# Normalised rows on ScalarE and experts added in pairs, in the last stage of a gated attention block

## The chip, the cores and the metric

One core of a Trainium2 chip runs the kernel. The metric is the device time of one execution in microseconds, from its start to its end; the change is measured against the kernel before on the same chip.

## The reference, cut to what matters

A block with 32 sequences of 128 rows and 128 features, all f32. First a cross attention of 16 heads without mask adds to x. Then a second part with causal self attention, two layer norms and eight experts, of which the two best by gate count for each row:

```python
attn_out = ctx @ out_proj_w.T + out_proj_b
x1 = _layer_norm(x + attn_out, ln1_w, ln1_b)
gates = softmax(x1 @ gate_w.T + gate_b)
top_gates, top_idx = the two largest gates of each row
expert_outputs = einsum('bsd,efd->bsef', x1, expert_w) + expert_b
moe_out = sum over the two of expert_outputs * top_gates
return _layer_norm(x1 + moe_out, ln2_w, ln2_b)
```

The output is x + tanh(g_ffn) times this. The last stage of the kernel computes what stands here.

## The kernel before

The work is in groups of G = 2 sequences, 16 groups (GROUPS). Two attention stages fill the time up to about 372 us; every engine then goes through the last stage, the functions `z_pe`, `z_act`, `z_dve`, `z_pool` and `z_sp`. The change touches this stage alone.

The stage is a software pipeline. `z_steps` (line 684) runs `body(s, c)` on each engine for s from -1 to 20, and `in_z(c, lag)` says whether the group s - lag is in a part of the pipeline. So one step handles five groups, each in another part: the group 0 steps back has its attention copied, projected and added to x, the group 1 step back is normalised and multiplied with the first four experts, the group 2 back is gated, the group 3 back is summed, and the group 4 back gets its final norm. On an engine the order within a step is the order in `body`, written by hand. Engines hand over by semaphores that count groups.

For one group, from first to last:

- ScalarE `fetch` (799) copies the attention; PE `transpose_att` (714), ScalarE `copy_att` (806), PE `project` (724).
- VectorE `attention_sum` (859 to 866) adds and makes mean and variance z_mv. GpSimd `factor1` calls `rstd_of` (646 to 650): variance plus EPS, then the power -0.5 into z_rstd.
- VectorE `normalise1` (875) makes z_n, one tensor_scalar a sequence, from z_h, mean and z_rstd. GpSimd `x1` (970, 975) multiplies by the norm's weights and adds its bias. PE `transpose_n` (731), ScalarE `copy_x1` (813) with the same weights as scale and bias, PE `logits` (740).
- PE `experts` (752) multiplies by eight experts, four (HALF) at a time: k = 0 into s_bank0 and st_bank0, k = 1 into s_bank1 and st_bank1.
- VectorE `shift_logits` (883, 886), ScalarE `gates_exp` (819), VectorE `gating` (895 to 907): the two largest exponentials over the sum, z_gates. PE `gates_t` (762) and ScalarE `copy_gates` (827) transpose them for the experts' biases.
- VectorE `experts` (922) sums the first four experts, each times its gate, onto x1. ScalarE `gate_experts` (837) scales the other four into z_gated, waiting for PE's sum of the group before (`z_yb`). PE `gated_sum` (771, 773) adds the biases and, by a product with the identity, the four z_gated of each sequence: 8 f32 matmuls a group at line 773, each seen as two pieces in the profile.
- VectorE `all_experts` (933 to 940) adds both halves and makes mean and variance again. GpSimd `factor2` calls `rstd_of`, VectorE `normalise2` (947) makes z_y, GpSimd `final` (982, 985, 990) makes the output, and SyncE stores it (700).

The two `body` functions whose order matters are those of VectorE: shift_logits, normalise1, normalise2, gating, experts, attention_sum, all_experts; and of ScalarE: gates_exp, copy_att, copy_x1, fetch, gate_experts, copy_gates. GpSimd has final, x1, factor1, factor2.

## Time and profile before

| what | value |
|---|---|
| median of three runs | 520.43 us (519.47 to 521.97) |
| the profiled execution's own time | 522.93 us |
| its span, first to last instruction | 521.1 us |
| busy in the span: PE, VectorE, ScalarE, GpSimd | 448.9, 385.2, 278.6, 323.7 us |
| mean granted TensorE clock | 0.95 of full speed |
| first instruction of the last stage (z_att) | 372.0 us |

The profile names the engines PE (PEld for its weight loads), DVE (VectorE), ACT (ScalarE), POOL (GpSimd) and SP (SyncE). Busy time of an engine is the union of its instructions, which overlap on all of them but GpSimd, so that a group's busy time can be less than count times mean. The bracket behind an instruction in the timeline is the idle time before it and what ended it. Names such as z_rstd_ with an underscore at the end belong to the second norm, those without to the first.

### The profile page before, as it was taken

How to read it: one execution, taken by the hardware profiler on the slowest of the kernel's cores; microseconds unless marked ns; L12 is line 12 of the kernel's file. 1: busy time of each engine (PE TensorE's matmuls, PEld its weight loads, DVE VectorE, ACT ScalarE, POOL GpSimd, SP SyncE). 2: the span in 40 equal slices, each digit the busy share in tenths (PEclk: the TensorE clock that was granted, in tenths of full speed). 3: DMA queues.
4: the chain of work that ended last, by engine and by line, in shares of the span. 5: the costliest groups of instructions: out<-in, count | busy, mean ns of one | idle time of the engine just before them, and what ended most of it. 6: DMA issues, size and time to landing. Idle time of an engine off the chain costs nothing.

```text
span 521.1 us, 15905 instructions
## 1 busy us (share of the span) xinstructions
PE 448.9 (86%) x5728; PEld 280.0 (54%) x5728; DVE 385.2 (74%) x1191; ACT 278.6 (53%) x693; POOL 323.7 (62%) x702
## 2 busy tenths in 40 slices
PE   0369788778888899999999999999789999999983
PEld 0134444444444456666666666666447666666652
DVE  6377878787786777767777777773269899999981
ACT  1126656666565665666656666666444554554530
POOL 1445654565468898887888878621044766667654
PEclk9999979888797999999999999999879999999995
DMA  4565775556343434344343443420000000000000
GB/s 108 127 170 132 183 173 128 125 141 152 94 108 95 103 91 98 86 106 110 96 98 85 105 115 93 98 70 10 3 0 11 12 20 23 10 22 11 23 20 20
DMA packets 88333, 42.70 MB, mean 82 GB/s; under 512 B 16312, under 2 KB 88128, under 8 KB 88256
## 3 DMA queue, kind: packets, MB, share of 16 engines
q1 hardware_dynamic: 79040, 39.59, 30.8%
q10 hardware_dynamic: 9216, 2.10, 2.0%
q8 instruction: 46, 0.75, 0.6%
q14 instruction: 31, 0.25, 0.2%
HBM read 5.75 MB, written 2.10 MB: 15 GB/s over the span
## 4 chain that ended last, share of the span: by engine, by line
PE 32%; DVE 20%; POOL 17%; issue 6%; ACT 2%; POOLq 0%; ACTq 0%; DVEq 0%
PE u_bank L421 6%; DVE z_acc L922 5%; PE s_bank L374 4%; PE s_bank L364 4%; POOL xn_all L238 4%; PE u_bank L773 2%; POOL rstd L233 2%; PE u_bank L434 2%; PE s_bank L752 2%; DVE nm L599 2%; POOL rc L256 2%; PE st_bank L752 2%; PE t_bank L346 2%; POOL z_rstd_ L650 2%; DVE stats L555 1%
## 5 line engine op out<-in xcount | busy, mean ns | idle before, releaser
L599 DVE TENSOR_REDUCE nm<-s_bank 128x4 f32<-128x512 f32 x256 | 173.1, 684 | 73.5 <-PE s_bank L374 71.7
L499 ACT ACTIVATE pt<-st_bank 128x512 f32<-128x512 f32 x256 | 150.0, 598 | 102.6 <-PE st_bank L374 60.4
L374 PE MATMUL s_bank<-qk 64*128 64x128 bf16 x1024 | 105.7, 231 | 11.3 <-DVE nm L599 7.7
L421 PE MATMUL u_bank<-pt,vaug 128*32 128x128 f32 x2048 | 113.8, 296 | 0.0
L374 PE MATMUL st_bank<-qk 64*128 64x128 bf16 x1024 | 106.4, 227 | 0.0
L374 PEld LDWEIGHTS s_bank<-qk 64*128 64x128 bf16 x1024 | 70.7, 99 | 39.2 <-issue 27.7
L374 PEld LDWEIGHTS st_bank<-qk 64*128 64x128 bf16 x1024 | 71.4, 98 | 0.4
L421 PEld LDWEIGHTS u_bank<-pt,vaug 128*32 128x32 f32 x2048 | 41.4, 111 | 29.0 <-issue 4.1
L364 PE MATMUL s_bank<-mqk,esel 64*128 64x256 bf16 x256 | 49.7, 274 | 0.4 <-ACT pt L499 0.4
L364 PE MATMUL st_bank<-mkq,esel 64*128 64x256 bf16 x256 | 49.7, 274 | 0.0
L280 POOL TENSOR_TENSOR part<-r,part 128x512 bf16<-128x512 f32 x32 | 37.1, 1159 | 2.7
L773 PE MATMUL u_bank<-z_gated,idf 128*128 128x128 f32 x256 | 38.4, 295 | 0.0
L837 ACT ACTIVATE z_gated<-s_bank,z_gates 128x128 f32<-128x128 f32 x64 | 18.2, 368 | 35.7 <-PE u_bank L773 35.7
L346 PE MATMUL t_bank<-idf,xp 128*128 128x128 f32 x32 | 9.2, 382 | 31.7 <-DVE xp L565 18.2
L752 PE MATMUL s_bank<-ewt,z_x_t 128*128 128x512 f32 x64 | 35.2, 632 | 0.3 <-DVE z_acc L922 0.3
L773 PEld LDWEIGHTS u_bank<-z_gated,idf 128*128 128x128 f32 x256 | 32.1, 197 | 4.0 <-issue 0.2
L752 PE MATMUL st_bank<-ewt,z_x_t 128*128 128x512 f32 x64 | 33.5, 605 | 0.0
L291 POOL TENSOR_SCALAR mst<-nm 128x16 bf16<-128x16 f32 x64 | 13.0, 203 | 32.1 <-DVE nm L599 29.2
L301 POOL TENSOR_TENSOR x_all<-x_all,ao 128x128 f32<-128x128 f32 x32 | 14.6, 455 | 28.3 <-DVE ao L616 27.2
L506 ACT ACTIVATE mts<-m_bank 128x128 bf16<-128x128 bf16 x64 | 17.8, 278 | 26.4 <-PE m_bank L429 26.2
L434 PE MATMUL u_bank<-idf,us 128*128 128x128 f32 x128 | 30.2, 321 | 0.5 <-ACT us L515 0.5
L648 POOL TENSOR_SCALAR z_ve<-z_mv 128x2 f32<-128x2 f32 x16 | 3.1, 191 | 43.4 <-DVE z_mv L866 43.3
(118 smaller groups left out, 904.3 us busy)
## 6 DMA issues: line engine op xcount, KB each, us to landing
qk<-part SPq DMA_DIRECT2D x224, 128.0 KB, 2.6
x_all<-x SPq DMA_DIRECT2D x16, 128.0 KB, 2.6
c_all<-ctx_in SPq DMA_DIRECT2D x16, 128.0 KB, 2.8
qk<-qrow SPq DMA_DIRECT2D x32, 64.0 KB, 2.1
qk<-mts ACTq DMA_DIRECT2D x64, 32.0 KB, 2.6
out<-z_o SPq DMA_DIRECT2D x16, 128.0 KB, 1.8
ewt<-exp_t SPq DMA_DIRECT2D x1, 512.0 KB
qk<-krow SPq DMA_DIRECT2D x4, 64.0 KB, 2.0
```

The lines of the kernel that those rows point to most:

```text
L238: pool.tensor_scalar(one(xn2_all, u * G + b), one(x_all, u * G + b), mv[u % 2][:, b, 0:1], rstd[:, b:b + 1], ALU.subtract, ALU.mult).then_ ...
L280: pool.tensor_tensor(part[u % 2][:, 2:2 * PARTS:PARTS, :], r32[:, :].rearrange("c (o t) -> c o t", o=2), part[u % 2][:, 1:2 * PARTS:PARTS, ...
L346: ins = pe.transpose(t_bank[:, i * P:(i + 1) * P], a, idf[:, :])
L364: pe.matmul(to, esel[rows, block, :], mask[rows, rows].unsqueeze(1).broadcast_to([64, HEADS, 64]), start=block == 0, stop=False, skip_grou ...
L374: return pe.matmul(bank[:, j * P:(j + 1) * P], k if keys_first else q, q if keys_first else k, start=not masked, stop=True, skip_group_che ...
L421: ins = pe.matmul(u_bank[b][32 * j:32 * j + 32, r * P:(r + 1) * P], v, pt[m % 4][:, j, :], start=half == 0, stop=half == 1, skip_group_che ...
L434: ins = pe.transpose(u_bank[q % 2][:, W + r * P:W + (r + 1) * P], us[q % 2][:, r * P:(r + 1) * P], idf[:, :])
L499: act.activation(pt[m % 4][:, :, :].rearrange("k j q -> k (j q)"), st_bank[m % 2][:, :], ACT.Exp).then_inc(ex, 1)
L599: dve.tensor_reduce(nm[q % 2][:, first:first + HEADS], s_bank[n % 2][:, :].rearrange("q (j k) -> q j k", j=HEADS), AX_X, ALU.max, negate=T ...
L752: ins = pe.matmul(e_bank[b][k][:, :], zx1t[i][:, b * P:(b + 1) * P], ewt[:, k * 512:(k + 1) * 512], start=True, stop=True)
L773: ins = pe.matmul(dst, idf[:, :], zyg[:, b, e, :], start=False, stop=e == HALF - 1)
L922: dve.scalar_tensor_tensor(out=zacc[i][e % 2][:, b, :], in0=e_bank[b][0][:, e * P:(e + 1) * P], scalar=zg[i][:, b, e:e + 1], in1=zacc[i][( ...
```

## The change

On ScalarE, `normalise1` and `normalise2` compute z * rstd + offset, with offset = -mean * rstd, as an activation with scale and bias taken per row; before, VectorE computed (z - mean) * rstd. GpSimd makes the offset in two more instructions of 128x2 behind each power. On VectorE, `gated_pairs` adds the four z_gated of each sequence two and two, in one instruction of 128x512 for both sequences, and PE sums two terms a sequence instead of four. `gate_experts` waits for this pair sum of the group before and no longer for PE's sum; `gated_pairs` waits for PE's sum of the group before. On ScalarE normalise1 stands first in the step, normalise2 behind copy_att; on VectorE gated_pairs stands where the two normalise functions stood.

```diff
--- before.py
+++ after.py
@@ -643,11 +643,14 @@
                         values(s + 2)
 
 
-        def rstd_of(pool, v_in, v_eps, r_out, semaphore, k):
-
-            pool.tensor_scalar(v_eps, v_in, 1.0, EPS, ALU.mult, ALU.add).then_inc(semaphore, 1)
+        def factor_and_offset(pool, mean_var, v_eps, r_out, mean_r, offset, semaphore, k):
+            pool.tensor_scalar(v_eps, mean_var[:, :, 1], 1.0, EPS, ALU.mult, ALU.add).then_inc(semaphore, 1)
             pool.wait_ge(semaphore, k + 1)
             pool.tensor_tensor(r_out, v_eps, mhalf[:, :], ALU.pow).then_inc(semaphore, 1)
+            pool.wait_ge(semaphore, k + 2)
+            pool.tensor_tensor(mean_r, mean_var[:, :, 0], r_out, ALU.mult).then_inc(semaphore, 1)
+            pool.wait_ge(semaphore, k + 3)
+            pool.tensor_scalar(offset, mean_r, -1.0, 0.0, ALU.mult, ALU.add).then_inc(semaphore, 1)
 
         def two(name, shape):
             return [sb(f"{name}{i}", shape) for i in range(2)]
@@ -655,7 +658,7 @@
         zo_t = two("z_att_t", [P, W])
         zh = two("z_h", [P, G, P])
         zst = two("z_stats", [P, G, 6]); zmv = two("z_mv", [P, G, 2]); zve = two("z_ve", [P, G]); zrs = two("z_rstd", [P, G])
-        zn = two("z_n", [P, G, P])
+        zn = two("z_n", [P, G, P]); znb = two("z_offset", [P, G]); zmr = two("z_mean_r", [P, G])
         zw = sb("z_nw", [P, G, P]); zx1 = two("z_x1", [P, G, P])
         zx1t = two("z_x1_t", [P, W])
         zl = sb("z_logit", [P, G, NE]); zm = sb("z_max", [P, G]); zp = sb("z_exps", [P, G, NE])
@@ -664,15 +667,15 @@
         zt = sb("z_top", [P, G, NE]); zg = two("z_gates", [P, G, NE]); zgt = two("z_gates_t", [NE, W])
         zacc = [[sb(f"z_acc{i}{j}", [P, G, P]) for j in range(2)] for i in range(2)]
         zst2 = sb("z_stats2_", [P, G, 6]); zmv2 = sb("z_mv2_", [P, G, 2]); zve2 = sb("z_ve2_", [P, G])
-        zrs2 = sb("z_rstd2_", [P, G]); zy = sb("z_y2", [P, G, P]); zyw = sb("z_yw", [P, G, P])
-        zsum = sb("z_x1_moe", [P, G, P]); zyg = sb("z_gated", [P, G, HALF, P]); zyb = sb("z_ywb", [P, G, P]); zo = two("z_o", [P, G, P])
+        zrs2 = sb("z_rstd2_", [P, G]); znb2 = sb("z_offset2_", [P, G]); zmr2 = sb("z_mean_r2_", [P, G]); zy = sb("z_y2", [P, G, P]); zyw = sb("z_yw", [P, G, P])
+        zsum = sb("z_x1_moe", [P, G, P]); zyg = sb("z_gated", [P, G, HALF, P]); zyp = sb("z_gated_pairs", [P, G, HALF // 2, P]); zyb = sb("z_ywb", [P, G, P]); zo = two("z_o", [P, G, P])
 
         z_at = sem("z_att_copied"); z_ot = sem("z_att_transposed"); z_otc = sem("z_att_t_copied")
         z_proj = sem("z_projected"); z_h = sem("z_ln1_steps"); z_rs = sem("z_rstd_steps")
         z_n = sem("z_normalised"); z_x1 = sem("z_x1_steps")
         z_nt = sem("z_n_transposed"); z_x1c = sem("z_x1_t_copied"); z_lg = sem("z_logits_ready")
         z_gate = sem("z_gate_steps"); z_exp = sem("z_gate_exp"); z_gt = sem("z_gates_transposed")
-        z_gtc = sem("z_gates_t_copied"); z_y = [sem(f"z_experts{k}") for k in range(2)]; z_yg = sem("z_experts_gated"); z_yb = sem("z_expert_bias")
+        z_gtc = sem("z_gates_t_copied"); z_y = [sem(f"z_experts{k}") for k in range(2)]; z_yg = sem("z_experts_gated"); z_yp = sem("z_gated_pairs_summed"); z_yb = sem("z_expert_bias")
         z_acc = sem("z_accumulated"); z_all = sem("z_all_summed_steps"); z_rs2 = sem("z_rstd2_steps"); z_y2s = sem("z_normalised2")
         z_fin = sem("z_final_steps"); z_out = sem("z_stored")
         H1 = 1 + 2 * G
@@ -765,12 +768,12 @@
             def gated_sum(g, gc):
                 i = gc % 2
                 pe.wait_ge(z_gtc, g + 1)
-                pe.wait_ge(z_yg, g + 1)
+                pe.wait_ge(z_yp, g + 1)
                 for b in range(G):
                     dst = u_bank[0][:, b * P:(b + 1) * P]
                     pe.matmul(dst, zgt[i][:, b * P:(b + 1) * P], ebs[:, :], start=True, stop=False)
-                    for e in range(HALF):
-                        ins = pe.matmul(dst, idf[:, :], zyg[:, b, e, :], start=False, stop=e == HALF - 1)
+                    for e in range(HALF // 2):
+                        ins = pe.matmul(dst, idf[:, :], zyp[:, b, e, :], start=False, stop=e == HALF // 2 - 1)
                 ins.then_inc(z_yb, 1)
 
             def body(s, c):
@@ -813,6 +816,24 @@
                 act.activation(zx1t[i][:, :], t_bank[:, 0:W], ACT.Identity, bias=l1bc[:, :],
                                scale=l1wc[:, :]).then_inc(z_x1c, 1)
 
+            def normalise1(g, gc):
+                i = gc % 2
+                act.wait_ge(z_rs, (g + 1) * 4)
+                if gc >= 2:
+                    act.wait_ge(z_nt, g - 1)
+                    act.wait_ge(z_x1, (g - 2) * 2 + 1)
+                for b in range(G):
+                    act.activation(zn[i][:, b, :], zh[i][:, b, :], ACT.Identity, bias=znb[i][:, b:b + 1],
+                                   scale=zrs[i][:, b:b + 1]).then_inc(z_n, 1)
+
+            def normalise2(g, gc):
+                act.wait_ge(z_rs2, (g + 1) * 4)
+                if gc >= 1:
+                    act.wait_ge(z_fin, (g - 1) * FIN + 1)
+                for b in range(G):
+                    act.activation(zy[:, b, :], zsum[:, b, :], ACT.Identity, bias=znb2[:, b:b + 1],
+                                   scale=zrs2[:, b:b + 1]).then_inc(z_y2s, 1)
+
             def gates_exp(g, gc):
                 act.wait_ge(z_gate, g * GATE + 2)
                 for b in range(G):
@@ -831,7 +852,7 @@
                 act.wait_ge(z_gate, (g + 1) * GATE)
                 act.wait_ge(z_y[1], g + 1)
                 if gc >= 1:
-                    act.wait_ge(z_yb, g)
+                    act.wait_ge(z_yp, g)
                 for b in range(G):
                     for e in range(HALF):
                         ins = act.activation(zyg[:, b, e, :], e_bank[b][1][:, e * P:(e + 1) * P], ACT.Copy,
@@ -839,10 +860,14 @@
                 ins.then_inc(z_yg, 1)
 
             def body(s, c):
+                if in_z(c, 1):
+                    normalise1(s - 1, c - 1)
                 if in_z(c, 2):
                     gates_exp(s - 2, c - 2)
                 if in_z(c, 0):
                     copy_att(s, c)
+                if in_z(c, 4):
+                    normalise2(s - 4, c - 4)
                 if in_z(c, 1):
                     copy_x1(s - 1, c - 1)
                 if in_z(c, -1):
@@ -864,16 +889,6 @@
                 dve.wait_ge(z_h, g * H1 + 1 + G)
                 for b in range(G):
                     dve.bn_aggr(zmv[i][:, b, :], zst[i][:, b, :]).then_inc(z_h, 1)
-
-            def normalise1(g, gc):
-                i = gc % 2
-                dve.wait_ge(z_rs, (g + 1) * 2)
-                if gc >= 2:
-                    dve.wait_ge(z_nt, g - 1)
-                    dve.wait_ge(z_x1, (g - 2) * 2 + 1)
-                for b in range(G):
-                    dve.tensor_scalar(zn[i][:, b, :], zh[i][:, b, :], zmv[i][:, b, 0:1], zrs[i][:, b:b + 1],
-                                      ALU.subtract, ALU.mult).then_inc(z_n, 1)
 
             per_seq = [P, G, NE]
 
@@ -924,6 +939,13 @@
                             scalar=zg[i][:, b, e:e + 1], in1=zacc[i][(e + 1) % 2][:, b, :] if e else zx1[i][:, b, :],
                             op0=ALU.mult, op1=ALU.add).then_inc(z_acc, 1)
 
+            def gated_pairs(g, gc):
+                dve.wait_ge(z_yg, g + 1)
+                if gc >= 1:
+                    dve.wait_ge(z_yb, g)
+                dve.tensor_tensor(zyp[:, :, :, :], zyg[:, :, 0:HALF // 2, :], zyg[:, :, HALF // 2:HALF, :],
+                                  ALU.add).then_inc(z_yp, 1)
+
             def all_experts(g, gc):
                 k = g * ALL
                 dve.wait_ge(z_yb, g + 1)
@@ -939,21 +961,11 @@
                 for b in range(G):
                     dve.bn_aggr(zmv2[:, b, :], zst2[:, b, :]).then_inc(z_all, 1)
 
-            def normalise2(g, gc):
-                dve.wait_ge(z_rs2, (g + 1) * 2)
-                if gc >= 1:
-                    dve.wait_ge(z_fin, (g - 1) * FIN + 1)
-                for b in range(G):
-                    dve.tensor_scalar(zy[:, b, :], zsum[:, b, :], zmv2[:, b, 0:1], zrs2[:, b:b + 1],
-                                      ALU.subtract, ALU.mult).then_inc(z_y2s, 1)
-
             def body(s, c):
                 if in_z(c, 2):
                     shift_logits(s - 2, c - 2)
-                if in_z(c, 1):
-                    normalise1(s - 1, c - 1)
-                if in_z(c, 4):
-                    normalise2(s - 4, c - 4)
+                if in_z(c, 3):
+                    gated_pairs(s - 3, c - 3)
                 if in_z(c, 2):
                     gating(s - 2, c - 2)
                     experts(s - 2, c - 2)
@@ -994,11 +1006,11 @@
                 pool.wait_ge(z_h, (g + 1) * H1)
                 if gc >= 2:
                     pool.wait_ge(z_n, (g - 1) * G)
-                rstd_of(pool, zmv[i][:, :, 1], zve[i][:, :], zrs[i][:, :], z_rs, g * 2)
+                factor_and_offset(pool, zmv[i], zve[i][:, :], zrs[i][:, :], zmr[i][:, :], znb[i][:, :], z_rs, g * 4)
 
             def factor2(g, gc):
                 pool.wait_ge(z_all, (g + 1) * ALL)
-                rstd_of(pool, zmv2[:, :, 1], zve2[:, :], zrs2[:, :], z_rs2, g * 2)
+                factor_and_offset(pool, zmv2, zve2[:, :], zrs2[:, :], zmr2[:, :], znb2[:, :], z_rs2, g * 4)
 
             def body(s, c):
                 if in_z(c, 4):
```

## Rows read from the trace of the kernel before

**Rows 1.** Windows of one step: busy us (instructions) per engine, clock, DMA
```profile
452.80:460.87 8.07, 8.07 (x44) 5.50 (x43) 7.42 (x36) 4.13 (x16) 5.43 (x10) 1.00 0.05 16
```

**Rows 2.** Chain of waits in the last stage: start us, us, what
```profile
399.61 0.44 PE m_bank L724 x4
...
407.61 0.45 PE m_bank L724 x4
...
448.69 2.16 DVE z_acc L922 x8
...
456.75 2.16 DVE z_acc L922 x8
```

**Rows 3.** Timeline of one step, VectorE: start us, us, engine, line
```profile
453.01 0.14 DVE L883 TENSOR_TENSOR z_logit<-u_bank,gbb 128x16 f32<-128x16 f32 x1
...
453.29 0.60 DVE L875 TENSOR_SCALAR z_n<-z_h,z_mv,z_rstd 128x128 f32<-128x128 f32 x2
...
454.22 0.60 DVE L947 TENSOR_SCALAR z_y<-z_x_moe,z_mv_,z_rstd_ 128x128 f32<-128x128 f32 x2 [0.32 <-POOL z_rstd_ L650]
...
454.74 0.23 DVE L895 MAX8 z_sorted<-z_exps 128x8 f32<-128x8 f32 x2
...
455.00 0.65 DVE L898 COPY z_two<-z_sorted 128x4 f32<-128x4 f32 x1
...
459.80 0.25 DVE L866 BATCH_NORM_AGGREGATE z_mv<-z_stats 128x2 f32<-128x6 f32 x2
```

**Rows 4.** Groups by line, whole span: busy us, mean ns, idle before
```profile
L599 DVE TENSOR_REDUCE nm<-s_bank 128x4 f32<-128x512 f32 x256 | 173.1, 684 | 73.5 <-PE s_bank L374 71.7 <-POOL mst L291 1.0
...
L773 PE MATMUL u_bank<-z_gated,idf 128*128 128x128 f32 x256 | 38.4, 295 | 0.0
...
L293 POOL TENSOR_TENSOR mr<-nm,mst 128x16 f32<-128x16 f32 x64 | 13.9, 218 | 5.3
...
L933 DVE TENSOR_TENSOR z_x_moe<-u_bank,z_acc 128x256 f32<-128x256 f32 x16 | 6.4, 399 | 4.6 <-PE u_bank L773 4.5
```

**Rows 5.** Timeline of the same step, GpSimd
```profile
453.45 0.73 POOL L650 TENSOR_TENSOR z_rstd_<-z_ve_,mhalf 128x2 f32<-128x2 f32 x1
...
454.90 0.72 POOL L982 TENSOR_TENSOR z_yw<-z_y,l2w 128x256 f32<-128x256 f32 x1 [0.72 <-DVE z_y L947]
...
458.02 0.73 POOL L975 TENSOR_TENSOR z_x<-z_nw,l1b 128x256 f32<-128x256 f32 x1
...
460.14 0.19 POOL L648 TENSOR_SCALAR z_ve<-z_mv 128x2 f32<-128x2 f32 x1 [1.39 <-DVE z_mv L866]
...
460.41 0.70 POOL L650 TENSOR_TENSOR z_rstd<-z_ve,mhalf 128x2 f32<-128x2 f32 x1
```

**Rows 6.** Timeline of the same step, ScalarE
```profile
453.93 0.47 ACT L819 ACTIVATE z_exps<-z_logit,z_max 128x8 f32<-128x8 f32 x2
...
456.26 0.56 ACT L813 ACTIVATE z_x_t<-t_bank,l1bc,l1wc 128x256 f32<-128x256 f32 x1 [1.59 <-PE t_bank L731]
...
456.73 0.41 ACT L799 ACTIVATE z_att<-c_all 128x256 f32<-128x256 f32 x1
...
459.35 1.14 ACT L837 ACTIVATE z_gated<-s_bank,z_gates 128x128 f32<-128x128 f32 x4 [2.21 <-PE u_bank L773]
```

**Rows 7.** Lines 898 and 905: duration ns min/median/max, first and last start
```profile
L898 DVE COPY z_two<-z_sorted x16: 170/645/650, 381.5 to 502.7; 128x4 f32<-128x4 f32 x16
...
L905 DVE TENSOR_TENSOR z_top<-z_exps,z_others x16: 174/375/382, 382.4 to 503.4; 128x16 f32<-128x16 f32 x16
```

**Rows 8.** Timeline of the last groups
```profile
506.41 1.14 ACT L837 ACTIVATE z_gated<-s_bank,z_gates 128x128 f32<-128x128 f32 x4 [4.05 <-PE u_bank L773]
...
507.31 0.25 DVE L940 BATCH_NORM_AGGREGATE z_mv_<-z_stats_ 128x2 f32<-128x6 f32 x2
...
508.83 0.48 PE L771 MATMUL u_bank<-ebs,z_gates_t 8*128 8x128 f32 x2 [1.55 <-ACT z_gates_t L827]
...
511.45 2.08 PE L773 MATMUL u_bank<-z_gated,idf 128*128 128x128 f32 x8
```

## The prediction

> **What bounds the kernel now.** I read the windows first, to see which engines are full, then the chain of waits, to see which of them sets the end, then the timeline of one step of the last stage, to price what is moved. The stage runs from 372 us to the end and makes 16 groups in a software pipeline. One step in its middle lasts 8.07 us [rows 1]: PE is busy all of it, VectorE 7.42, GpSimd 5.43 and ScalarE 4.13. Two engines are thus nearly full at once. The chain says the same: up to 412 us it runs through PE, its project matmuls 8.00 us apart; later it runs through VectorE, its expert sums 8.06 apart [rows 2]. PE and VectorE each set the same period, so taking work from one alone gains nothing. The change takes from both, and what is left is a loop of handoffs.
>
> Within a step (t = 453.01, start of the logits' sum) [rows 3]: VectorE makes the first normalised rows at 453.29, waits for z_rstd_, makes the second at 454.22, starts the gating at 454.74 and the expert sums 2.01 later, at 456.75 [rows 2]. From there to the next step's logits (461.08) are 4.33 us.
>
> **The change, part by part.**
> PE loses 8 of its 16 pieces a group (an f32 matmul shows as two): 128 of the 256, whose busy time is 38.4 us in all [rows 4]. Half of it over 16 groups is 1.2 us a step, and PE's work becomes 8.07 - 1.2 = 6.9 us.
>
> VectorE loses both pairs of tensor_scalar and the wait between them: 454.74 - 453.29 = 1.45 us. It gains one sum of 128x512 (the four gated experts of each sequence, two and two, for both sequences at once). No row has a two-tensor sum so wide; the reduce over 512 columns takes 0.684 and z_x_moe over 256 takes 0.399 [rows 4]. These bound it at 0.68 and 2 x 0.40 = 0.80; I take 0.69, as its width is that of the reduce. VectorE's own work becomes 8.07 - 1.45 + 0.69 = 7.3 us.
>
> GpSimd gains two small instructions for each factor. The nearest is mr, 128x16, 0.218 us [rows 4]; z_ve, with 2 columns, takes 0.19 [rows 5]. With the 0.08 between dependent instructions (460.14 + 0.19 to 460.41) [rows 5] I take 0.29 + 0.27 = 0.56, between 0.54 and 0.60. A factor then takes 0.27 + 0.78 + 0.56 = 1.61 us until the next one can start, and 1.53 to the end of its last instruction.
>
> ScalarE gains four activations of 128x128 with two pointer operands. ScalarE has room, so their price is latency. z_x_t, with two pointers and 256 columns, takes 0.56 and the next starts 0.47 after it; z_gated, with one pointer and 128 columns, has starts (1.14 - 0.37) / 3 = 0.26 apart [rows 6]. For a pair, starts lie between 0.52 and 0.94 and the end between 0.61 and 1.03; between these I take starts 0.72 in all, and 0.82 to the end. The Trainium skill (ScalarE: Activation LUTs, What ACT_TABLE_LOAD costs) states 186 ns + 0.833 ns a column, 93 ns for each pointer operand and an overlap of 93 ns; that gives 0.77 and 0.87, and would add 0.05 to the sum below, which goes by the rows.
>
> What stands behind the new waits: the exponentials of the gating now queue behind normalise1 on ScalarE, and normalise1 waits for GpSimd's four instructions. VectorE's gating waits for the exponentials, and the attention sum that feeds the next factor comes after gating and experts. So the price of a handoff comes back in every step: attention sum, factor1, normalise1, exponentials, gating, experts, next attention sum. The copy of the attention also queues behind, so PE's project starts late, but PE has over 1 us to spare. normalise2 waits for factor2 and holds copy_x1, fetch and the gated experts behind it; these have room, since ScalarE had idle stretches of 2.21 us before z_gated [rows 6].
>
> **The port.** Two tiny VectorE instructions with both operands in SBUF, the copy z_two and the difference z_top, take 0.170 and 0.174 at best, 0.645 and 0.375 as a rule [rows 7]. In the step, z_two (455.00) ends at 455.65 while GpSimd's z_yw ends at 455.62 [rows 3, 5]; it waited for GpSimd. The new sum reads two SBUF operands for 0.69 us, so it may hold up GpSimd as well. The trace has no row for that side: bounds are 0 and the sum's whole 0.69. The Trainium skill (SBUF — State Buffer, SBUF: two separate sides) calls the shared pair "an exclusive lock, not a bandwidth split", either side blocking the other for a whole instruction; by it the wait exists, and without it the result would be the first rival's. The row agrees for VectorE waiting, none shows GpSimd waiting. I take the wait as real, since the small cases show one.
>
> **The sum for a step.** z_mv of the attention sum ends at 460.05 and GpSimd starts 0.09 later [rows 3, 5], if it is free. GpSimd's own loop, without port waits, is: factor1 1.61, factor2 1.53, handoff 0.04 (z_rstd_ ends 454.18, z_y starts 454.22), ScalarE's pair 0.82, to z_yw 0.08, from z_yw to the end of x1 454.90 to 458.75 = 3.85, and 0.08 to the next factor [rows 3, 5]: 8.01 us. GpSimd is thus nearly full itself. In a step of 8.27, the result below, its x1 ends at t + 7.7, and factor1 starts 0.4 later than the 0.09 would have it. The product mean*rstd, 1.05 after that start, is then ready at 0.5 after the next t, while the pair sum runs (from t + 0.28 to t + 0.97). I let the product end 0.10 after the sum (between 0.03, as z_two did, and 0.22, the whole instruction). Then offset 0.27, handoff 0.04, two normalised 0.72, exponentials 0.47 [rows 6] and handoff 0.04: gating starts at t + 2.61. Gating shrinks, because GpSimd is waiting for ScalarE at that time: z_two falls by 0.48 and z_top by 0.20, so 2.01 becomes 1.33 (between 1.33 and 2.01). Step: 2.61 + 1.33 + 4.33 = 8.27, or 0.20 more than before. With every term at its low end it is 7.96; with every one at its high end 9.4, of which 0.68 is a gating held up as before and 0.42 the dearest activations. I don't expect these together, and take 8.8 as the upper side of the range.
>
> **Ends of the stage.** At the start, factor1 is on the path once: +0.56, and +0.2 for ScalarE's pair against VectorE's 0.60 = +0.8. At the end, z_gated of the last group waited 4.05 us for PE's previous sum [rows 8]; that wait becomes one for the pair sum, which comes early. The last pair sum then queues behind the previous group's statistics, ending 507.56 (about 0.2 earlier now), and adds 0.7: PE starts at 508.1 instead of 508.83. That last gated sum took until 513.53, or 4.70 us; the bias pieces keep about 1.2, and half of the other 3.5 goes, 1.75. Factor and pair then cost 0.56 + 0.2. Together -0.7 - 1.75 + 0.76 = -1.7. Net of both ends: -0.9 us (between +0.5, if the last sum halves only in part, and -2.5, if the last groups run freer, having fewer stages beside them).
>
> Between them lie about 12 steps under the loop, 16 less four in which the pipeline fills: 12 x 0.20 = +2.4. Sum +1.5. The profiled execution, 522.93 us with a span of 521.10, becomes 524.4; it stands 2.5 above the median of the three runs, 520.43, which becomes 521.9. A measurement can tell about 0.5%, 2.6 us, from no change.
>
> **Rivals.**
> First, GpSimd isn't held by the sum. The step is then GpSimd's own loop, 8.01, or 7.76 with the small instructions and ScalarE's pair at their lower price. 12 x -0.06 - 0.9 = -1.6, or 12 x -0.31 - 0.9 = -4.6: 518.8 to 515.8. For it: no row shows GpSimd held, and its instructions of 128x256 keep 0.72 [rows 5]. Against: VectorE's two small ones are held at the median [rows 7].
> Second, the other side: the port wait adds in full to the POOL loop. If the power instruction also holds the port, the pair sum starts only when it ends, and the product waits for the whole sum: 8.01 + 0.69 = 8.70. 12 x 0.63 - 0.9 = +6.7: 527.1. The step from which this side decides is 8.07 + (2.6 + 0.9) / 12 = 8.36. For it: GpSimd's loop is the tightest. Against: the z_n pair (one tensor from SBUF each, so only a hint) took 0.60 beside z_rstd_ and isn't drawn out [rows 3, 5].
> Third, the handoffs hide after all, and VectorE's own 7.3 us sets the step: 12 x -0.77 - 0.9 = -10.1: 510.3. Against: gating can't start before the exponentials, and these follow normalise1; the order is in the code. The change would do nothing of what it says if PE's row of pieces did not halve; nothing speaks for that.
>
> **Chances.** Forecast 0.45 (of it 0.32 within 0.5%, 0.10 slower, 0.03 faster), first rival 0.27 (0.17 faster, 0.10 within), second 0.23 (all slower), third 0.05 (faster). Faster 0.25, same 0.42, slower 0.33. The range, 515.5 to 527.0, takes in the first rival and the forecast's bounds, and most of the second; it leaves out the third and the second's far end. The forecast's own is 519.5 to 525.
>
> **What would show it.** u_bank from z_gated: 128 pieces. PE busy under 90% of a step. VectorE idle some 1.6 us a step, its gating released by ScalarE's z_exps. z_two and z_top near 0.17. GpSimd's product in the first factor longer than 0.22, or a gap before it, when the pair sum runs. Steps of 8.27 us. Wrong would be: z_yw or the offset without delay and steps under 8; PE with gaps that lower its granted clock in the stage, which no term here counts; or activations of 128x128 outside 0.37 to 0.56.

## The result, and the profile after

The changed kernel takes 529.72 us (median of 4 runs, 527.32 to 532.58), the kernel before, on the same chip, 519.95 (519.47 to 521.97). The ratio on record, 1.016 with a 95% interval of 1.012 to 1.021, is not the plain quotient of these two medians, which would be 1.019. The forecast was 521.9, with a range up to 527.0: the changed kernel is slower than the one before, and lies outside the range. The profiled execution took 530.40 us with a span of 528.4, against 522.93 and 521.1.

The first part of the page of the changed kernel, busy time and share of the span, shows the work moved as the change says. Against the kernel before PE has 10 us less, VectorE 16 less, ScalarE 26 and GpSimd 17 more:

```profile
span 528.4 us, 15744 instructions
...
PE 438.8 (83%) x5600; PEld 265.0 (50%) x5600; DVE 369.4 (70%) x1143; ACT 304.5 (58%) x757; POOL 340.6 (64%) x766
```

In windows, one step in the middle (columns as in [rows 1]) is 8.27 us. No engine is full now, where PE was full before:

```profile
430.74:439.01 8.27, 7.41 (x35) 4.50 (x34) 6.28 (x33) 5.71 (x18) 6.38 (x13) 1.00 0.05 17
```

The timeline of this step on VectorE and GpSimd answers to [rows 3, 5], that of ScalarE to [rows 6]:

```profile
430.74 0.19 POOL L647 TENSOR_SCALAR z_ve<-z_mv 128x2 f32<-128x2 f32 x1
...
431.01 0.70 POOL L649 TENSOR_TENSOR z_rstd<-z_ve,mhalf 128x2 f32<-128x2 f32 x1
...
431.49 0.68 DVE L946 TENSOR_TENSOR z_gated_pairs<-z_gated 128x512 f32<-128x512 f32 x1
431.79 0.44 POOL L651 TENSOR_TENSOR z_mean_r<-z_mv,z_rstd 128x2 f32<-128x2 f32 x1
...
432.32 0.19 POOL L653 TENSOR_SCALAR z_offset<-z_mean_r 128x2 f32<-128x2 f32 x1
432.55 0.88 ACT L826 ACTIVATE z_n<-z_h,z_offset,z_rstd 128x128 f32<-128x128 f32 x2 [0.81 <-POOL z_offset L653]
...
433.33 0.47 ACT L840 ACTIVATE z_exps<-z_logit,z_max 128x8 f32<-128x8 f32 x2
...
433.84 0.24 DVE L910 MAX8 z_sorted<-z_exps 128x8 f32<-128x8 f32 x2 [1.66 <-ACT z_exps L840]
433.92 0.19 POOL L653 TENSOR_SCALAR z_offset_<-z_mean_r_ 128x2 f32<-128x2 f32 x1
...
434.11 0.17 DVE L913 COPY z_two<-z_sorted 128x4 f32<-128x4 f32 x1
...
434.14 0.88 ACT L834 ACTIVATE z_y<-z_x_moe,z_offset_,z_rstd_ 128x128 f32<-128x128 f32 x2
...
434.71 0.18 DVE L920 TENSOR_TENSOR z_top<-z_exps,z_others 128x16 f32<-128x16 f32 x1
...
435.10 0.73 POOL L994 TENSOR_TENSOR z_yw<-z_y,l2w 128x256 f32<-128x256 f32 x1 [0.99 <-ACT z_y L834]
```

Read it from the pair sum at 431.49. GpSimd's z_mean_r begins 0.30 later and takes 0.44 us where it takes 0.20 when free: it ends at 432.23, 0.06 behind the sum. Then come z_offset, ScalarE's z_n, the exponentials, and VectorE, idle for 1.66 us, starts the gating at 433.84, which is t + 2.61 (t, the start of the logits' sum, is at 431.23). z_two and z_top take 0.17 and 0.18, against the 0.645 and 0.375 of [rows 7], as GpSimd waits for z_y at that time. From the gating to the sums are 1.35 us, and GpSimd's z_yw starts at 435.10 after 0.99 us of idling.

The chain of waits of one step (start us, us, what; each piece was released by the one above it) runs through GpSimd and ScalarE's z_y, no longer through VectorE as in [rows 2]:

```profile
426.27 0.49 ACT z_y L834
...
426.83 0.72 POOL z_yw L994
...
429.93 0.73 POOL z_x L987
...
431.01 0.71 POOL z_rstd L649
...
431.79 0.45 POOL z_mean_r L651
...
432.87 0.70 POOL z_rstd_ L649
...
434.55 0.49 ACT z_y L834
```

The rest is seen from the power instruction z_rstd of each group. From z_att's start to that of the fourth group the stage takes 23.5 us before (372.05 to 395.51) and 26.9 after (370.80 to 397.73); from there to the sixteenth 97.2 (to 492.72) and 101.6 (to 499.31); from there to the end 28.4 and 29.1. That is +3.5, +4.4 and +0.7, together +8.55 us before rounding; the stages ahead, which the change doesn't touch, ended 1.2 earlier (they end anywhere from 368.8 to 373.3 us in the profiles of this document). So the profiles differ by 7.5 us; the medians differ by 9.8, and what the rest is wasn't traced. Of the 4.4, 12 steps at 8.28 instead of 8.08 make 2.4, and the other 2.0 fall in one place. There the steps are 8.55, 9.94 and 8.42 us long. The last two lie at a lowered clock and are 1.8 us over 8.28. The first, 0.27 over, is something else: the pair sum starts there at 448.32, just ahead of z_mean_r at 448.35, and z_mean_r takes 0.70 us instead of 0.44; in e4 and e14 below, at full clock, the same step is 8.56 and 8.53. Windows of that place, and of the last groups (columns as in [rows 1]; the last but two is the granted clock, of which 1.00 is 2.4 GHz and 0.50 is 1.2):

```profile
450.00:455.00 5.00, 4.14 (x24) 3.52 (x23) 4.14 (x22) 4.71 (x16) 3.64 (x7) 0.84 0.00 0
455.00:460.00 5.00, 5.00 (x10) 2.35 (x11) 2.14 (x11) 0.81 (x3) 3.52 (x9) 0.50 0.11 31
500.00:505.00 5.00, 4.24 (x22) 2.55 (x20) 3.18 (x18) 3.85 (x14) 3.37 (x9) 0.96 0.01 2
505.00:510.00 5.00, 4.29 (x7) 1.93 (x8) 2.67 (x11) 0.89 (x5) 3.74 (x7) 0.50 0.09 26
```

### The profile page after: what moved, and what is told of

Same layout as the page of the kernel before. It is cut to its first block, busy times and chain, and to the rows that moved or that the text cites. A ratio compares the mean times of both kernels' runs of the same rounds, so it can differ in the third digit from the quotient of the medians.

```text
span 528.4 us, 15744 instructions
## 1 busy us (share of the span) xinstructions
PE 438.8 (83%) x5600; PEld 265.0 (50%) x5600; DVE 369.4 (70%) x1143; ACT 304.5 (58%) x757; POOL 340.6 (64%) x766
## 4 chain that ended last, share of the span: by engine, by line
POOL 30%; PE 27%; DVE 9%; issue 8%; ACT 4%; POOLq 0%; ACTq 0%; DVEq 0%
PE u_bank L421 6%; PE s_bank L364 4%; POOL xn_all L238 4%; PE s_bank L374 4%; POOL rstd L233 2%; PE u_bank L434 2%; POOL rc L256 2%; PE t_bank L346 2%; DVE nm L599 2%; POOL z_rstd L649 2%; POOL z_yw L994 2%; POOL z_ywb L997 2%; POOL z_o L1002 2%; POOL z_rstd_ L649 2%; PE s_bank L755 2%
## 5 line engine op out<-in xcount | busy, mean ns | idle before, releaser
L374 PE MATMUL s_bank<-qk 64*128 64x128 bf16 x1024 | 103.8, 228 | 12.4 <-DVE nm L599 8.8
L421 PE MATMUL u_bank<-pt,vaug 128*32 128x128 f32 x2048 | 112.3, 293 | 0.0
L374 PE MATMUL st_bank<-qk 64*128 64x128 bf16 x1024 | 104.5, 224 | 0.0
L374 PEld LDWEIGHTS s_bank<-qk 64*128 64x128 bf16 x1024 | 69.7, 98 | 39.0 <-issue 26.9
L374 PEld LDWEIGHTS st_bank<-qk 64*128 64x128 bf16 x1024 | 70.2, 97 | 0.4
L755 PE MATMUL s_bank<-ewt,z_x_t 128*128 128x512 f32 x64 | 38.4, 684 | 1.3 <-DVE z_acc L937 1.2
L755 PE MATMUL st_bank<-ewt,z_x_t 128*128 128x512 f32 x64 | 35.4, 636 | 0.0
L291 POOL TENSOR_SCALAR mst<-nm 128x16 bf16<-128x16 f32 x64 | 13.2, 206 | 32.1 <-DVE nm L599 29.1
L275 POOL TENSOR_SCALAR part<-r 128x512 bf16<-128x512 f32 x32 | 19.9, 621 | 14.1 <-DVE r L575 12.2
L238 POOL TENSOR_SCALAR xn_all<-x_all,mv,rstd 128x128 f32<-128x128 f32 x32 | 25.4, 798 | 1.8
L429 PE MATMUL m_bank<-idb,mst 128*128 128x128 bf16 x64 | 15.0, 235 | 13.7 <-POOL mst L297 12.8
L364 PEld LDWEIGHTS s_bank<-mqk,esel 64*128 64x128 bf16 x256 | 14.1, 94 | 22.5 <-issue 16.0
```

Of the source, the lines that this page charges most:

```text
L238: pool.tensor_scalar(one(xn2_all, u * G + b), one(x_all, u * G + b), mv[u % 2][:, b, 0:1], rstd[:, b:b + 1], ALU.subtract, ALU.mult).then_ ...
L275: pool.tensor_scalar(part[u % 2][:, 1:2 * PARTS:PARTS, :], r32[:, :].rearrange("c (o t) -> c o t", o=2), 1.0, 0.0, ALU.mult, ALU.add).then ...
L364: pe.matmul(to, esel[rows, block, :], mask[rows, rows].unsqueeze(1).broadcast_to([64, HEADS, 64]), start=block == 0, stop=False, skip_grou ...
L374: return pe.matmul(bank[:, j * P:(j + 1) * P], k if keys_first else q, q if keys_first else k, start=not masked, stop=True, skip_group_che ...
L421: ins = pe.matmul(u_bank[b][32 * j:32 * j + 32, r * P:(r + 1) * P], v, pt[m % 4][:, j, :], start=half == 0, stop=half == 1, skip_group_che ...
L755: ins = pe.matmul(e_bank[b][k][:, :], zx1t[i][:, b * P:(b + 1) * P], ewt[:, k * 512:(k + 1) * 512], start=True, stop=True)
```

## The experiments

The step is the distance of the z_rstd instructions in the middle; times are medians of 4 runs (10 of e15, 6 of e14), each ratio is that of the record, with its 95% interval against the kernel before on the same chip, whose median was 519.95, 521.46, 521.09 or 521.77 us as the runs went on.

| run | what | us | ratio | step us |
|---|---|---|---|---|
| changed kernel | | 529.72 | 1.016 (1.012 to 1.021) | 8.28 |
| e1_sum_twice | pair sum made twice | 536.62, one run | | 8.60 at full clock |
| e2_extra_psum | a second sum, one operand in PSUM | 529.47, one run | | 8.36 and 8.56 in turn |
| e3_order | exponentials ahead of z_n | 528.10 | 1.014 (1.010 to 1.018) | 8.35 |
| e4_ballast | identity products in PE's gap | 529.21 | 1.014 (1.009 to 1.019) | 8.28 |
| e5_four_terms | no pair sum | 526.82 | 1.011 (1.005 to 1.018) | 8.19 |
| e6_pairs_only | norms on VectorE | 525.94 | 1.011 (1.003 to 1.019) | 8.40 |
| e10_x1_first | x1 ahead of final | 544.03 | 1.041 (1.032 to 1.050) | 9.21, five of 9.45 to 9.72 |
| e16_x1_first_filled | e10, gap filled | 539.08 | 1.034 (1.029 to 1.039) | 9.22 |
| e11_both_orders | e3 and e10 | 508.47 | 0.977 (0.971 to 0.982) | 7.09 |
| e15_orders_four | e11, no pair sum | 523.21 | 1.002 (0.999 to 1.005) | 8.00 |
| e12_both_neg | e11, one instruction less on GpSimd | 513.98 | 0.985 (0.980 to 0.990) | 7.18 and 7.62 in turn |
| e14_filled | PE's gaps filled, also at the end | 527.56 | 1.011 (1.007 to 1.015) | 8.28 |

### Does the pair sum hold up GpSimd? e1_sum_twice and e2_extra_psum

```diff
                 if gc >= 1:
                     dve.wait_ge(z_yb, g)
+                dve.tensor_tensor(zdup[:, :, :, :], zyg[:, :, 0:HALF // 2, :], zyg[:, :, HALF // 2:HALF, :], ALU.add)
                 dve.tensor_tensor(zyp[:, :, :, :], zyg[:, :, 0:HALF // 2, :], zyg[:, :, HALF // 2:HALF, :],
```

> The pair sum is made twice (first into a tile that nothing reads), output unchanged. VectorE was idle 1.66 us behind its one pair sum (684 ns) before the gating, so the second sum has room on VectorE itself. Theory: two SBUF operands hold up GpSimd, so z_mean_r, which took 0.44 us instead of 0.20 beside the one sum, and z_offset behind it take or start about 0.6 to 0.7 us later, and a step of 8.28 us becomes 8.9 to 9.0. Rival, GpSimd isn't held by the sum: z_mean_r stays at 0.44 or below and the step at 8.28.

The lines of z_mean_r and z_offset in e1 (ns min/median/max):

```profile
L651 POOL TENSOR_TENSOR z_mean_r<-z_mv,z_rstd x16: 194/451/710, 376.2 to 505.3; 128x2 f32<-128x2 f32 x16
L653 POOL TENSOR_SCALAR z_offset<-z_mean_r x16: 191/511/604, 376.4 to 505.8; 128x2 f32<-128x2 f32 x16
```

z_mean_r is held by the first sum and z_offset by the second, 0.51 instead of 0.19 at the median. In steps at full clock the step is 8.60, 0.32 longer. The time of 536.62 has more in it than 12 x 0.32: steps of up to 10.29 us at a lowered clock. The hold is real; I had it at 0.6 to 0.7 a step, as if the second sum were added whole, but z_mean_r and its handoff had already used half of it.

```diff
+                if gc < GROUPS - 1:
+                    dve.wait_ge(z_y[0], g + 2)
+                    dve.tensor_tensor(zdup[:, :, :, :], e_bank[0][0][:, :].rearrange("q (b e d) -> q b e d", b=G, e=HALF // 2),
+                                      zyg[:, :, HALF // 2:HALF, :], ALU.add)
                 dve.tensor_tensor(zyp[:, :, :, :], zyg[:, :, 0:HALF // 2, :], zyg[:, :, HALF // 2:HALF, :],
```

> As e1_sum_twice, but the extra sum of 128x512 reads one operand from PSUM and one from SBUF; the result is stored nowhere that is read. It takes as long on VectorE (0.65 to 0.70 us), so it costs VectorE the same. Theory (two SBUF operands are what holds GpSimd): the extra sum holds nothing; the real pair sum now comes 0.7 us later, and meets whatever GpSimd does then, so z_mean_r is at 0.20 and the step stays within 0.3 us of 8.28. Rival, any VectorE work of that length at that place delays the loop: 8.9 us, as in e1.

The extra sum also waits for PE's k = 0 experts, whose PSUM bank it reads. One step of e2, timeline:

```profile
431.60 0.69 DVE L949 TENSOR_TENSOR z_dup<-s_bank,z_gated 128x512 f32<-128x512 f32 x1
431.86 0.20 POOL L651 TENSOR_TENSOR z_mean_r<-z_mv,z_rstd 128x2 f32<-128x2 f32 x1
...
432.14 0.19 POOL L653 TENSOR_SCALAR z_offset<-z_mean_r 128x2 f32<-128x2 f32 x1
432.20 0.68 DVE L951 TENSOR_TENSOR z_gated_pairs<-z_gated 128x512 f32<-128x512 f32 x1
...
432.41 0.53 POOL L647 TENSOR_SCALAR z_ve_<-z_mv_ 128x2 f32<-128x2 f32 x1
```

Beside a sum with one operand in PSUM both small instructions run at 0.20 and 0.19; the real sum behind it holds the next one, z_ve_, 0.53 instead of 0.19. So it is the sum with two SBUF operands that holds GpSimd, and it holds whichever instruction it meets. In e6_pairs_only that is the power instruction z_rstd_, 1.05 us at the median instead of 0.73.

### Which loop sets the step? e3_order, e10_x1_first, e11_both_orders

```diff
             def body(s, c):
-                if in_z(c, 1):
-                    normalise1(s - 1, c - 1)
                 if in_z(c, 2):
                     gates_exp(s - 2, c - 2)
                 if in_z(c, 0):
                     copy_att(s, c)
+                if in_z(c, 1):
+                    normalise1(s - 1, c - 1)
```

> On ScalarE the gates' exponentials and the copy of the attention come before the first normalised rows. Theory (GpSimd's own loop of factors, final and x1 with ScalarE's second normalised rows in it sets 8.28 us): VectorE's 1.66 us of waiting for z_exps moves elsewhere, the step stays between 8.0 and 8.3 us, and the gain is in the filling of the pipeline, which took 3.5 us more than before: 2 to 3 us less than the changed kernel. Rival (the exponentials queued behind the normalised rows set the step): the step falls to between 7.3 and 7.6 us and the time by 8 us or more.

The step is 8.35, not shorter, and the chain still goes through GpSimd's factors, final and x1 and through z_y: with the exponentials out of the queue nothing is gained, so that queue alone wasn't the bound. The swap also moves the pair sum against GpSimd's work. z_mean_r is free now (0.194 to 0.198 us in all 16 groups), but the sum meets z_x or z_ve instead; in this step it waits for z_x, which had started first, and then holds z_ve:

```profile
437.07 0.72 POOL L987 TENSOR_TENSOR z_x<-z_nw,l1b 128x256 f32<-128x256 f32 x1
437.40 0.95 DVE L946 TENSOR_TENSOR z_gated_pairs<-z_gated 128x512 f32<-128x512 f32 x1
437.88 0.52 POOL L647 TENSOR_SCALAR z_ve<-z_mv 128x2 f32<-128x2 f32 x1
```

z_ve takes 0.52 instead of 0.19 here, and in most other steps z_x takes 1.05 instead of 0.72. GpSimd's loop without the hold is thus 8.35 - 0.33 = 8.02 us in e3 and 8.27 - 0.24 = 8.03 in the changed kernel: the same loop, held at another instruction. The filling took 1.7 us less, since the second group's attention copy no longer waits behind z_n. The time fell by 1.6 us where I expected 2 to 3, which the scatter of either (526.66 to 529.40 and 527.32 to 532.58) can't tell apart.

```diff
             def body(s, c):
-                if in_z(c, 4):
-                    final(s - 4, c - 4)
                 if in_z(c, 1):
                     x1(s - 1, c - 1)
+                if in_z(c, 4):
+                    final(s - 4, c - 4)
```

> The changed kernel with two lines swapped on GpSimd: x1 of one group comes before final of the other, so that GpSimd works on x1 while ScalarE makes z_y. Theory (GpSimd's loop of 8.28 holds 1.0 us of idling for z_y, which this fills): its loop falls to 7.3, and the next loop takes over, pair sum, offset, z_n, z_exps, gating, at 7.9 to 8.1 us a step; time 2 to 4 us below the changed kernel, 525 to 528. Rival (GpSimd's order is not what binds): steps stay at 8.28.

It went the other way: 9.21 us a step. The timeline of e10 shows why:

```profile
430.90 0.73 POOL L982 TENSOR_TENSOR z_nw<-z_n,l1w 128x256 f32<-128x256 f32 x1
430.94 0.71 DVE L913 COPY z_two<-z_sorted 128x4 f32<-128x4 f32 x1
...
431.71 0.72 POOL L987 TENSOR_TENSOR z_x<-z_nw,l1b 128x256 f32<-128x256 f32 x1
...
432.40 0.72 POOL L994 TENSOR_TENSOR z_yw<-z_y,l2w 128x256 f32<-128x256 f32 x1
432.50 0.65 DVE L922 TENSOR_TENSOR z_gates<-z_top,z_rsum 128x16 f32<-128x16 f32 x1
...
435.45 2.07 PE L755 MATMUL s_bank<-ewt,z_x_t 128*128 128x512 f32 x2 [1.10 <-DVE z_acc L937]
...
437.95 0.60 POOL L653 TENSOR_SCALAR z_offset<-z_mean_r 128x2 f32<-128x2 f32 x1
```

GpSimd no longer waits for z_y (it idles later, 1.89 us before z_ve), and with that wait went the quiet in which VectorE had its gating: z_two takes 0.71, z_gates 0.65, z_top 0.38, each until GpSimd's instruction ends, and z_offset is held by the pair sum, 0.60. All four are on the loop of exponentials, gating, experts, attention sum, factor, z_n. My 7.9 to 8.1 had taken the gating at 1.35 us there; here it is 2.56. In about half of the steps, as in this one, PE then runs its k = 0 experts at a granted clock of 0.50 after a wait of 0.55 or 1.10 us, and the chain goes through them: z_gates_t comes late, z_n and the exponentials stand behind it on ScalarE, and in the gating that follows (440.72 to the sums) z_two is free, 0.17. Such steps are as long as the others or longer, so the clock looks like a cause too; e16 below tests it.

> Both orders: x1 before final on GpSimd, and on ScalarE exponentials and attention copy before z_n. The two loops of the theory are both shortened; left are VectorE's 7.3 us and PE's 6.9 of work: steps of 7.3 to 7.6 us, 12 x -0.9 against the changed kernel plus 1.3 from the filling: 517 to 520, at or below the kernel before. Rival (one more loop, or clock dips that grow with PE's gaps): steps of 8.0 or more, or dips, and 524 or more.

Both swaps together (no other edit) give 508.47 us, 12.6 below the kernel before in the same set of runs (ratio 0.977, 0.971 to 0.982) and 21 below the changed one. The windows of one step of e11, and its chain:

```profile
422.53:429.63 7.10, 7.10 (x38) 4.53 (x36) 6.29 (x33) 5.49 (x20) 6.20 (x14) 1.00 0.06 18
```

```profile
422.88 0.96 PE s_bank L755 x2
423.84 0.86 PE st_bank L755 x2
...
425.14 0.86 PE s_bank L755 x2
426.00 0.86 PE st_bank L755 x2
426.85 0.45 PE m_bank L727 x4
```

PE is busy for all of the 7.10 us and the chain is PE's alone. With z_n behind them the exponentials no longer wait for the factors, and GpSimd no longer waits for z_y; each swap alone leaves the other loop. The step came out 0.2 below the range I gave, because VectorE's work, which I had at 7.3, is 6.29: the 7.3 was taken off the step's 8.07, in which VectorE was busy 7.42, and had the held gating in it. PE's own work is 7.10, where I had 6.9. The time is 8.5 us below my 517 to 520: beside the steps, the end of the stage takes 25.7 us instead of 29.1, which I hadn't counted.

### What is each part worth? e5_four_terms, e6_pairs_only, e15_orders_four

e5 takes the pair sum out of the changed kernel (PE sums z_gated as before, ScalarE waits for z_yb); e15 is the same edit on e11. e6 gives both normalise functions back to VectorE, behind gated_pairs, and takes the two added instructions from GpSimd.

```diff
-                pe.wait_ge(z_yp, g + 1)
+                pe.wait_ge(z_yg, g + 1)
...
-                    for e in range(HALF // 2):
-                        ins = pe.matmul(dst, idf[:, :], zyp[:, b, e, :], start=False, stop=e == HALF // 2 - 1)
+                    for e in range(HALF):
+                        ins = pe.matmul(dst, idf[:, :], zyg[:, b, e, :], start=False, stop=e == HALF - 1)
...
-                if in_z(c, 3):
-                    gated_pairs(s - 3, c - 3)
```

e6, on VectorE:

```diff
                 if in_z(c, 3):
                     gated_pairs(s - 3, c - 3)
+                if in_z(c, 1):
+                    normalise1(s - 1, c - 1)
+                if in_z(c, 4):
+                    normalise2(s - 4, c - 4)
```

> Only the part with the normalised rows: they stay on ScalarE, but the pair sum is taken out and PE sums four terms a sequence as before. PE has 8.0 us of work a step, and no pair sum meets GpSimd. Theory (GpSimd's loop: 8.28 less the 0.24 that the pair sum holds z_mean_r): steps of 8.05 to 8.1 us, z_mean_r 0.20, no clock dips as PE has no gaps, so the middle costs nothing, and what is left is the filling, +3 us: 523 to 525. Rival (the pair sum costs nothing, the moved rows all): steps stay 8.28 and the time is above 527.

> Only the part with the pairs: VectorE makes both normalised rows again and GpSimd only the factors, and the pair sum is added in front of them. VectorE's work becomes 8.07 + 0.69 = 8.76 us less the 0.32 in which it waited for z_rstd_: steps of 8.4 to 8.8 us, PE with gaps, 525 to 529 with the filling as before (no change there). Rival (PE's saving matters more than VectorE's load): steps of 8.0 us or less.

> e11_both_orders with PE summing four terms a sequence and no pair sum. In e11 the step is 7.09 us and PE is busy all of it, so PE binds, and four terms add 1.1: steps of 8.15 to 8.2 us, 12 x 1.1 more: 520 to 523. So the pair sum is worth 13 us once the orders let PE bind. Rival (e11 is fast for its orders alone): steps under 7.6 us and 515 or less.

e5: steps of 8.19, z_mean_r 0.20, no lowered clock in the middle; the chain is PE's, 0.19 above the 8.00 of e15, because project gets its attention copy late, behind z_n (0.64 us in the chain instead of 0.45). The filling costs 3.4 us, about the 3.5 of the changed kernel, and the time is 2 us above what I gave. e6: 8.40, the lower end, with places at a lowered clock, and a filling 1.9 us longer than before, where I had expected none (not followed up). So each part alone costs about 1%. e15: steps of 8.00, 0.15 under what I gave, as the four terms cost PE 0.9 us a step and not 1.1, and a time that can't be told from the kernel before. The same pair sum that gains nothing in the changed kernel is worth 523.2 - 508.5 = 14.7 us under the other orders (14.1 with each set against its own runs of the kernel before), since there PE's work is what binds.

### Is GpSimd's work still a bound? e12_both_neg

```diff
             pool.tensor_tensor(r_out, v_eps, mhalf[:, :], ALU.pow).then_inc(semaphore, 1)
             pool.wait_ge(semaphore, k + 2)
-            pool.tensor_tensor(mean_r, mean_var[:, :, 0], r_out, ALU.mult).then_inc(semaphore, 1)
-            pool.wait_ge(semaphore, k + 3)
-            pool.tensor_scalar(offset, mean_r, -1.0, 0.0, ALU.mult, ALU.add).then_inc(semaphore, 1)
+            pool.tensor_tensor(offset, mean_r, r_out, ALU.mult).then_inc(semaphore, 1)
...
+                dve.tensor_scalar(zmr[i][:, :], zmv[i][:, :, 0], -1.0, 0.0, ALU.mult, ALU.add).then_inc(z_h, 1)
```

> e11_both_orders with the offset made by one GpSimd instruction instead of two; VectorE makes the negated means of 128x2 behind its statistics. GpSimd's loop gets 0.54 us shorter, VectorE's work 0.3 longer, to 7.6. Theory (PE's 7.09 us bind in e11 and neither of the others): no gain, the same within 0.5%, or up to 4 us slower if VectorE becomes the bound. Rival (GpSimd still binds): steps below 7.0 us.

No gain, as the theory has it, but 5.5 us slower than e11, more than it allowed: steps of 7.18 and 7.62 in turn, and a tail of 28.6 us instead of 25.7. The trace shows VectorE as the new bound: the chain in the middle is VectorE's alone, without a wait for another engine. In every second step its z_gates starts together with GpSimd's z_nw (both at 434.67) and takes 0.75 us; in the others it takes 0.17. The longer steps are these, 7.62. In the tail PE runs the last k = 0 experts at a clock of 0.50, 2.07 and 1.56 us for the two matmul pairs, where e11 has 1.11 and 1.02.

### The clock: e4_ballast, e16_x1_first_filled, e14_filled

```diff
             def project(g, gc):
                 i = gc % 2
-                pe.wait_ge(z_otc, g + 1)
                 if gc >= 1:
                     pe.wait_ge(z_h, (g - 1) * H1 + 1)
+                for e in range(4):
+                    pe.matmul(m_bank[:, W:W + P], idf[:, :], ewt[:, 0:P], start=True, stop=True)
+                pe.wait_ge(z_otc, g + 1)
```

> PE makes four identity products of 128x128 into unused columns of the projection's PSUM bank while it waits for the transposed attention, so that it is as busy as before the change (8.0 us a step); nothing reads them. Theory (steps of 9.9 us around 450 to 460 us and the tail at half clock come from a lowered clock after PE's gaps): the granted clock stays at 1.00 from 390 us on, all steps are 8.28, and the time falls by 2 to 4 us against the changed kernel, to about 526, with less scatter between runs. Rival (the clock falls for another reason, or the added work lies on the path): the clock dips remain and the time is the same or longer.

In its profile the clock is 1.00 from 390 to 500 us and no step is above 8.56 after the filling, so the 1.8 us at a lowered clock are gone; but the filling is 1.1 us longer, where the clock is low and the products are added too, the end of the stage is as long as in the changed kernel (29.2), and the median is 529.21 where I expected about 526, not to be told from the changed kernel's.

e16 adds three such products (`fill_t` makes them), into t_bank, ahead of the k = 0 experts of e10:

```diff
                     logits(s - 1, c - 1)
+                    if c >= 3:
+                        fill_t(3)
                     experts(s - 1, c - 1, 0)
```

> e10_x1_first, in whose steps PE waits 1.10 us for z_acc and then runs the expert matmuls at a granted clock of 0.50 (2.07 us instead of 1.12), with three identity products of 128x128 (0.8 us) into unused columns of t_bank in that gap; nothing reads them. Theory (a gap of that length before the experts is what lowers the clock, and the lowered clock lies on the path through k = 0 experts, gates' transpose, z_gates_t, z_n, z_exps): the clock stays 1.00, steps fall from 9.2 to between 8.0 and 8.4 us, and the time from 544 to about 530. Rival (the clock has nothing to do with the gap, or the chain is long without it): steps stay above 9 us.

I had expected steps of 8.0 to 8.4 and about 530 us. The clock is 1.00 from 390 to 525 us, the experts take 1.12 instead of 2.07, and the step is still 9.22, with z_two at 0.72, z_top at 0.38, z_gates at 0.65 and z_offset at 0.60 in the middle steps. So the lowered clock didn't set e10's step: where it is on the chain, the held gating, which takes its place when the clock is kept, is as long. It costs e10 the steps of 9.45 to 9.72, which e16 doesn't have, about 2 us in all in the two profiles.

e14 puts three products ahead of the projection from the fifth step on, and five into t_bank ahead of the last group's k = 0 experts:

```diff
+                if gc >= 4:
+                    fill(3)
...
                     logits(s - 1, c - 1)
+                    if c == GROUPS:
+                        fill_t(5)
                     experts(s - 1, c - 1, 0)
```

> The changed kernel with PE's gaps filled by identity products that nothing reads: three a step ahead of the projection from the fifth step on, and five ahead of the last k = 0 experts, before which PE waited 1.03 us and then ran at 0.50. Theory: no dip in the middle (2.0 us less) and the end of the stage shorter by 2 to 3 us: 525 to 526, and runs closer together. Rival (the dips are not the cause, as the ballast of e4 left the median alone): 529 or more.

The windows of e14 at the same two places:

```profile
450.00:460.00 10.00, 9.81 (x49) 6.30 (x48) 7.43 (x38) 6.22 (x20) 7.86 (x17) 1.00 0.05 16
500.00:505.00 5.00, 4.57 (x24) 2.73 (x22) 3.14 (x20) 3.77 (x12) 3.43 (x9) 1.00 0.01 3
505.00:510.00 5.00, 5.00 (x22) 2.68 (x21) 3.96 (x22) 2.38 (x9) 4.11 (x8) 1.00 0.10 28
```

The experts of the last group at 506.14 take 1.10 and 1.02 us; in the changed kernel, after a gap of 1.03 us, PE ran them at 0.50 from 505.70 and they took 2.07 and 1.91. No step in the middle shows a lowered clock, and the end of the stage takes 27.1 us instead of 29.1. From z_att to the end its profiled execution is 153.7 us long, 3.9 less than the changed kernel's 157.6. The median, 527.56, is above the 525 to 526 that I expected. It agrees in direction (ratio 1.011 against 1.016), but the intervals overlap, so the profile shows it and the times only lean that way. Other traces bear out the end: the first of the last k = 0 experts takes 1.97 to 2.08 us in e1, e2, e3, e4, e6 and e12, in which PE has gaps ahead of it, and 1.10 to 1.12 in e5, e11 and e15, in which PE is full. For the middle one profile each doesn't show that the filled gaps are why the clock stayed: e2, whose gaps are not filled and are 0.60 and 1.49 us in turn, also keeps it at 1.00 from 390 to 500 us.

## Why the prediction was wrong, point by point

The steps of the prediction that failed are the two costs under "Ends of the stage", and a term that was named and put at nothing: gaps of PE that lower its clock. The step of the loop itself held.

**The step was right.** Forecast 8.27, measured 8.27 to 8.28. Pair sum 0.684 (taken 0.69), z_mean_r until 0.06 after it (0.10), factor chain 0.27, 0.78, 0.29, 0.27 as taken, ScalarE's pair 0.78 to the next start and 0.88 to its end (0.72 and 0.82), gating at t + 2.61 and 1.35 long (1.33). The single terms are off by up to 0.06 us, and that these cancel to 0.00 is luck. The hold of GpSimd, inferred from two tiny instructions of VectorE, is shown by e1 and e2. The Trainium skill (ScalarE: Activation LUTs, What ACT_TABLE_LOAD costs) gave 0.77 and 0.87 for ScalarE's pair, and the trace agrees with it to 0.01. Its rule of an exclusive lock (SBUF — State Buffer, SBUF: two separate sides) agrees with e1 (z_offset 0.51 us instead of 0.19), e2 (z_mean_r free at 0.20 beside the sum with an operand in PSUM) and e6 (z_rstd_ 1.05 instead of 0.73). Twelve steps gave the +2.4 us of the forecast. What is not as I put it is the loop named: the sum ran along VectorE's chain, and it is GpSimd's own, 8.03 us (8.01 forecast) + 0.24 of hold, that closes at 8.27. VectorE's chain comes out as long because z_mean_r and z_n tie it to GpSimd, so e3, which shortens only VectorE's, gains nothing in the step.

**The filling was wrong: +0.8 forecast, +3.5 measured.** I costed factor and z_n of the first group only. In the code the copy of the second group's attention stands behind z_n on ScalarE, and PE's project ahead of the transpose of z_n. ScalarE and PE, timeline of the changed kernel:

```profile
376.74 0.88 ACT L826 ACTIVATE z_n<-z_h,z_offset,z_rstd 128x128 f32<-128x128 f32 x2 [4.05 <-POOL z_offset L653]
377.52 0.36 ACT L809 ACTIVATE z_att_t<-t_bank 128x256 f32<-128x256 f32 x1
...
377.94 1.22 PE L727 MATMUL m_bank<-wo,z_att_t 128*128 128x128 f32 x4 [3.85 <-ACT z_att_t L809]
...
378.95 0.63 PE L734 MATMUL t_bank<-idf,z_n 128*128 128x128 f32 x2
```

z_att_t waits until 377.52 for z_n; PE projects at 377.94 and only then transposes z_n at 378.95. Before, both had been done at 375.18 and 375.61, while the factor was made. From the first z_rstd to the second are 5.36 us instead of 3.32, and from the third to the fourth 8.67 instead of 7.72; e3 and e15, with the exponentials first, have 7.72 and 7.73 there. "PE has over 1 us to spare" was true of the middle and was used for the start. e3 gets 1.7 us of it back.

**The end was wrong: -1.7 forecast, +0.7 measured.** The sum was for a clock as before. The pieces did halve, but PE's k = 0 experts of the last group ran at 0.50, on the path: 505.70 to 509.28, where before it was 499.36 to 501.18. e14 keeps the clock there and gets 27.1 us against 28.4 before, so -1.3: the forecast less 0.4. Its last gated sum takes 3.8 us (514.55 to 518.35), where the forecast had 4.70 - 1.75 = 2.95.

**The middle had a term that wasn't priced: 2.0 us.** I named gaps that lower the granted clock as what would make the forecast wrong, and said that no term counts them. The lowered clock at 453 to 460 us is 1.8 of it; the rest is the longer hold in the step ahead. That PE's gaps lowered the clock there is not shown, as said under e14. In the sum 2.7 for the filling, 2.4 for the end and 2.0 for this place make 7.05 us before rounding, which is all of the difference between +1.5 and the +8.55 of the profiles.

**Terms that were off without mattering here.** PE was to save 1.2 us a step; e15 and e11 show 0.9, 8.00 less 7.09. VectorE's own work was put at 7.3 and is 6.28, and the third rival's 7.3 with it. In the upper side of 9.4 the dearest activations are 0.22 above the value taken; the 0.42 given there is their distance from the low end.

**The rivals.** The first (no hold) is refuted by e1, with e2 beside it, and by z_mean_r's 0.44. The second came nearest in time, 527.1, but for another reason: no step of 8.70 is there. The third didn't occur here; e11 shows that under other orders the handoffs do hide, but what sets the step then is PE's 7.10 us.

## What to carry to other kernels

Moving work off a full engine gains only if the handoffs it adds don't close a longer loop; count the loop through every engine's hand-written order, including the idle time that an engine spends waiting inside it. When two loops are about equally long, one reordering shows nothing or harm and both together show everything, so try the pair before judging the part. Price the filling and the end of a pipeline by their own queues and at the clock that PE will have there, not by the slack of the middle.
